# VectorE's order in the top-k attention of a Macaron block: where the sign word, the limits and the reciprocals stand

## The reference

```python
x = x + 0.5 * ffn(layernorm(x))       # x: 8 x 512 x 256
x = x + attn(layernorm(x))
x = x + 0.5 * ffn(layernorm(x))

def attn(x):                          # H = 16 heads of 64, 4 memory keys, TOPK = 64
    q, k, v = x @ Wq, x @ Wk, x @ Wv  # in heads; memory keys and values put in front of k and v
    q, k = l2norm(q), l2norm(k)
    dots = einsum('bhid,bhjd->bhij', q, k) * 10
    dots = einsum('hg,bgij->bhij', W_pre_th, dots)           # heads mixed before
    dots = where(causal, mask_value, dots)
    vk = top_k(dots, TOPK)[0][..., -1:]                      # the 64th largest of each row
    dots = where(dots < vk, mask_value, dots)
    attn = softmax(dots)
    attn = einsum('hg,bgij->bhij', W_post_th, attn)          # heads mixed after
    out = einsum('bhij,bhjd->bhid', attn, v) * head_scale
    return (out * sigmoid(x @ Wg + bg)) @ Wo
```

## Time and profile before

| | us |
|---|---|
| median of 3 runs | 2283.63 |
| lowest and highest of them | 2280.85 and 2287.51 |
| the profiled execution: time | 2286.81 |
| its span in the trace | 2285.0 |
| outside the span (2286.81 - 2285.0) | 1.81 |
| TensorE busy | 2040.8 (89%) |
| VectorE busy | 1765.2 (77%) |
| ScalarE busy | 1602.4 (70%) |
| GpSimd busy | 938.0 (41%) |

### The profile page before, as it was taken

How to read it: one execution, slowest core, us unless ns; L and a number is a source line. 1 busy time by engine, 2 the same in 40 slices (tenths; PEclk the granted TensorE clock), 3 DMA queues, 4 the chain that set the end, 5 groups by cost and what they waited for, 6 DMA issues and landing times. The chain is left out here.

```text
span 2285.0 us, 55636 instructions
## 1 busy us (share of the span) xinstructions
PE 2040.8 (89%) x16059; PEld 1325.7 (58%) x16060; DVE 1765.2 (77%) x6818; ACT 1602.4 (70%) x4676; POOL 938.0 (41%) x2739
## 2 busy tenths in 40 slices
PE   7995799899989998899899988998899889974997
PEld 3433456666666666666666666666666666663433
DVE  6565389968996899689968996899689958984346
ACT  4442589858985888589768875897689768951542
POOL 3001455454544554555355435553554356321000
PEclk9997799999999999999999999999999999997998
DMA  6002012111211121112111211121112101302002
GB/s 180 0 0 88 18 46 63 44 26 44 63 44 26 44 63 44 26 44 63 44 27 44 63 44 26 45 62 44 26 45 63 44 24 48 70 24 89 1 0 74
DMA packets 113219, 104.72 MB, mean 46 GB/s; under 512 B 34448, under 2 KB 110864, under 8 KB 112912
## 3 DMA queue, kind: packets, MB, share of 16 engines
q1 hardware_dynamic: 108000, 96.65, 16.6%
q10 hardware_dynamic: 4912, 4.46, 0.6%
HBM read 19.14 MB, written 12.71 MB: 14 GB/s over the span
## 5 line engine op out<-in xcount | busy, mean ns | idle before, releaser
L1054 PE MATMUL bankC<-R,E 128*128 128x128 f32 x2560 | 352.0, 287 | 46.9 <-POOL R L1416 46.9
L1054 PEld LDWEIGHTS bankC<-R,E 128*128 128x128 f32 x2560 | 338.3, 202 | 85.1 <-POOL R L1416 51.8
L1038 PE MATMUL bankB<-raw,mixpre 128*128 128x76 f32 (+37 forms) x1024 | 354.7, 434 | 20.4 <-DMA raw<-SC 20.3
L1254 ACT ACTIVATE S<-bankB,aim_first 128x68 f32<-128x68 f32 (+56 forms) x456 | 232.8, 514 | 87.8 <-PE bankB L1038 87.2
L1514 DVE TENSOR_SCALAR_CACHE_REDUCE S<-S,minus_thr 128x68 f32<-128x68 f32 (+56 forms) x456 | 217.7, 514 | 94.1 <-POOL minus_thr L1400 93.5
L1391 POOL TENSOR_TENSOR S<-S,diagmask 128x8 f32<-128x8 f32 x512 | 116.6, 233 | 409.1 <-ACT S L1254 353.0
L1568 DVE SCALAR_TENSOR_TENSOR E<-S,limit,E 128x68 f32<-128x68 f32 (+56 forms) x456 | 234.1, 549 | 37.6 <-ACT E L1280 9.0
L1416 POOL TENSOR_SCALAR R<-mixpost,rinv 128x128 f32<-128x128 f32 x512 | 187.6, 379 | 183.8 <-DVE rinv L1572 183.4
L1027 PE MATMUL bankD<-KT,QT 64*64 64x132 f32 (+8 forms) x2304 | 190.5, 405 | 66.5 <-ACT SC L1243 37.4
L1280 ACT ACTIVATE E<-S,nmax 128x12 f32<-128x12 f32 (+56 forms) x512 | 241.7, 535 | 0.0
L1080 PEld LDWEIGHTS bankM<-PT,V 128*64 128x64 f32 x5120 | 180.3, 138 | 97.9 <-issue 90.5
(11 more groups left out here) (178 smaller groups left out, 3927.7 us busy)
## 6 DMA issues: line engine op xcount, KB each, us to landing
X_first<-in_L_attn_x_dram ACTq DMA_DIRECT2D x8, 512.0 KB, 9.7
x<-X_first SPq DMA_DIRECT2D x8, 512.0 KB, 2.9
xt<-x SPq DMA_DIRECT2D x32, 128.0 KB, 2.3
x<-xt SPq DMA_DIRECT2D x32, 128.0 KB, 2.4
X_last<-x SPq DMA_DIRECT2D x8, 512.0 KB, 6.6
out_dram<-X_last SPq DMA_DIRECT2D x8, 512.0 KB, 2.8
raw<-SC SPq DMA_DIRECT2D x8, 258.0 KB, 3.0
raw<-SC SPq DMA_DIRECT2D x8, 254.0 KB, 3.0
```

The source lines that it names most:

```text
L1038: last = nc.tensor.matmul(bankB[n % 2][:, 0:wide(n)], W.mixpre[:, :], raw[n % RAWS][:, 0:wide(n)], start=True, stop=True)
L1054: last = nc.tensor.matmul(bankC[n % 2][:, jb * P:(jb + 1) * P], E[n % EBUFS][:, jb * P:(jb + 1) * P], R[n % RBUFS][:, :], start=True, stop ...
L1254: nc.scalar.activation(S[n % SBUFS][:, 0:wide(n)], src, ACT.Identity, bias=W.aim_first[:, group(n)]).then_inc(S_out, 1)
```

## The change

Four things are moved on VectorE's list; no other engine's list is touched.

1. The sign word (flip, L1527) was the first instruction of select_pair(n0), behind both row maxima. It becomes sides_pair(n0) and stands between row_max(n0+2) and row_max(n0+3).
2. The limit of both groups (L1556, one instruction) becomes one instruction for each group, each behind a wait for its own picked; the masked sum of a group waits for its own limit.
3. The reciprocal of a pair (L1572) was the last instruction of select_pair(n0). It becomes invert_pair(n0), and is called in the next iteration, behind row_max(n0+4) and before the next pair's sign word. So it also stands behind whatever follows select_pair(n0) in its own iteration: gate_half, ln_apply, residual, squares, mark_batch.
4. The reciprocal of the last pair stands behind the loop, so behind the last mark_batch. Its wait for R_ready (ring of 16) is put at the reciprocal too.

```diff
--- before.py
+++ after.py
@@ -1516,17 +1516,32 @@
                 else:
                     nc.vector.reduce_max(rmax[:, col(n)], row, axis=AX.X).then_inc(max_done, 1)
 
+            flipped, kept_sum = {}, {}
+
+            def sides_pair(n0):
+
+                ranked = ranked_in(n0)
+                if ranked:
+                    cols = ring(ranked)
+                    dve.wait_ge(side_done, ranked_upto(ranked[-1]))
+                    flipped[n0] = step(nc.vector.tensor_scalar(flip[:, cols], side[:, cols].bitcast(I32), 31, 0x7FFFFFFF,
+                                                               ALU.arith_shift_right, ALU.bitwise_or))
+
+            def invert_pair(n0):
+
+                both = (n0, n0 + 1)
+                dve.wait_ge(tk, kept_sum[n0])
+                if n0 >= RING:
+                    dve.wait_ge(R_ready, n0 - RING + 2)
+                nc.vector.reciprocal(rinv[:, ring(both)], rsum[:, ring(both)]).then_inc(E_ready, 2)
+
             def select_pair(n0):
 
                 both = (n0, n0 + 1)
                 ranked = ranked_in(n0)
                 at = {}
                 if ranked:
-                    cols = ring(ranked)
-                    dve.wait_ge(side_done, ranked_upto(ranked[-1]))
-                    flipped = step(nc.vector.tensor_scalar(flip[:, cols], side[:, cols].bitcast(I32), 31, 0x7FFFFFFF,
-                                                           ALU.arith_shift_right, ALU.bitwise_or))
-                    dve.wait_ge(tk, flipped)
+                    dve.wait_ge(tk, flipped[n0])
                     for n in ranked:
                         w = group_width(n)
                         at[n] = step(nc.vector.tensor_scalar(
@@ -1552,10 +1567,11 @@
                             out=picked[n % 2][:, :], in0=W.iotaM[:, :], scalar=order[:, col(n)], in1=top[n % 2][:, :],
                             op0=ALU.is_equal, op1=ALU.mult,
                             accum_out=key[:, parity(n), n % GPB:n % GPB + 1]).then_inc(picked_done, 1)
-                    dve.wait_ge(picked_done, ranked_upto(ranked[-1]))
-                    limited = step(nc.vector.tensor_tensor(
-                        limit[:, cols].bitcast(I32), key[:, parity(n0), in_batch(ranked)].bitcast(I32), flip[:, cols],
-                        ALU.bitwise_xor))
+                    for n in ranked:
+                        dve.wait_ge(picked_done, ranked_upto(n))
+                        at[n] = step(nc.vector.tensor_tensor(
+                            limit[:, col(n)].bitcast(I32), key[:, parity(n), n % GPB:n % GPB + 1].bitcast(I32),
+                            flip[:, col(n)], ALU.bitwise_xor))
                 for n in both:
                     w = group_width(n)
                     dve.wait_ge(exp_done, n + 1)
@@ -1563,13 +1579,12 @@
                         dve.wait_ge(R_ready, n - RING + 1)
                     least = MASKED / 2
                     if n in ranked:
-                        dve.wait_ge(tk, limited)
+                        dve.wait_ge(tk, at[n])
                         least = limit[:, col(n)]
                     at[n] = step(nc.vector.scalar_tensor_tensor(
                         out=E[n % EBUFS][:, 0:w], in0=S[n % SBUFS][:, 0:w], scalar=least, in1=E[n % EBUFS][:, 0:w],
                         op0=ALU.is_ge, op1=ALU.mult, accum_out=rsum[:, col(n)]))
-                dve.wait_ge(tk, at[n0 + 1])
-                nc.vector.reciprocal(rinv[:, ring(both)], rsum[:, ring(both)]).then_inc(E_ready, 2)
+                kept_sum[n0] = at[n0 + 1]
 
             def mark_batch(i):
 
@@ -1595,8 +1610,13 @@
             squares(1, 1)
             for n0 in range(0, NG, 2):
                 t, g = divmod(n0, GPT)
-                if 2 <= n0 and n0 + 2 < NG:
+                more = 2 <= n0 and n0 + 2 < NG
+                if more:
                     row_max(n0 + 2)
+                if n0:
+                    invert_pair(n0 - 2)
+                sides_pair(n0)
+                if more:
                     row_max(n0 + 3)
                 if g == 2 and t + 2 < NT:
                     ln_stats(t + 2)
@@ -1613,6 +1633,7 @@
                     squares(t + 1, 1)
                 if (n0 + 2) % GPB == 0:
                     mark_batch(n0 // GPB)
+            invert_pair(NG - 2)
             gate_half(NU - 2)
             gate_half(NU - 1)
             residual(NT - 2)
```

## The result

The changed kernel takes 2246.57 us (median of 4 runs, 2243.7 to 2247.8), the kernel before 2282.93 beside it. The ratio is 0.9836, with a 95% interval of 0.9818 to 0.9854: 36.4 us or 1.6% faster. The forecast was 12.5 us faster, 2271.1, with a range down to 2259. The sign was right, the size a third of what came. One of the six runs of e5_middle took 2637.43 us at a mean granted clock of 0.739, the five others 2271.79 to 2273.34 at 0.953 to 0.954; its ratio goes by those five.

What follows compares the result with a forecast made beforehand. VectorE was taken to set the time only in four iterations at each of 7 batch ends and the kernel's last 12; 9.1 + 3.4 = 12.5 us off 2286.81 gave 2274.3, as median 2271.1, range 2259 to 2283.

Steps and rivals of the forecast that it cites:

- the rival by which the time would rise to 2288: VectorE's list: order is free, only instruction count matters; one added limit an iteration costs 4.4 us; chance 0.05.
- the late R of group 58: Batch end: the put-off reciprocal gives TensorE R 0.76 us later, which fits into its wait for k of 1.87 to 2.92.
- the mask of group 5: GpSimd at a batch end: the later reciprocal just fits before this mask; up to 0.3 us a batch if it doesn't.
- an iteration: VectorE, each iteration: removed 0.34 + 0.20 + 0.05, added 0.11 + 0.15, so 0.33 us saved; ends 0.19 and 0.45.
- The slower rival: TensorE leads more and waits for the late reciprocal: 5.3 us at batch ends, 4.8 in wide tiles, 2294; chance 0.11.
- In tiles 1 and 2 nothing is gained: Middle of a batch: no gain; a later R taken as nothing, up to 0.3 us a tile on the bad side.
- a VectorE that works faster finds no thresholds to work on: Tile 2: VectorE and TensorE have no gaps to speak of, so VectorE's gain becomes longer threshold waits; size nothing.
- I take nothing: TensorE's clock at batch starts: loss of up to 1.7 us goes in five batches, counted as nothing; 8.5 kept as an end.
- the batches without it don't come to group 58 earlier in any regular way (they lose the clock elsewhere): Batches without the clock loss at their start: reason given for counting no time from its end.
- the clock comes along: Rival, TensorE's clock at batch starts: shorter waits end the clock loss, 8.5 us more, 2263; chance 0.12.
- the batch end: Group 58 to the squares: squares 1.35 us earlier; over 7 batch ends 5 x 1.35 + 1.11 + 1.25 = 9.1 us.
- The last batch: From group 42 of the last batch VectorE leads: 3.8 us gained, 0.3 to 0.4 back, net 3.4.

Runs made afterwards that it cites:

- e5_middle: All three moves only in the pairs of groups 0 to 54 of each batch, old order in 56 to 62, against the kernel before: ratio 0.9954.
- e3_limit: Only the limits split, one per group; reciprocal and sign word as in the kernel before: ratio 0.9915 to it.
- e8_recip58: The changed kernel with the reciprocal of groups 58 and 59 left right behind their masked sums: ratio 0.9839 to the kernel before.
- e9_last: All three moves only in the last batch (groups 448 to 511), the rest as in the kernel before: ratio 0.9957 to it.
- e7_delay: The changed kernel with four idle VectorE multiplications in front of the squares at each batch end: ratio 0.9906 to the kernel before.
- e10_tile2: All three moves only in pairs 32 to 47 (tile 2) of batches 0 to 6, against the kernel before: ratio 0.9977.
- e12_after: The changed kernel run again, unchanged, as a control: ratio 0.9851 to the kernel before.

## Why the prediction was wrong

**What held.** VectorE sets the time from group 58 to the squares; the squares come earlier, TensorE's wait for k shrinks and goes; the order of VectorE's list matters, not its count (the rival by which the time would rise to 2288 fell with e3_limit); no new wait of TensorE for R in tiles 1 and 2; the late R of group 58 fits into the wait for k; the mask of group 5 costs at most 0.12 us a batch (starts without a loss take 12.52 to 12.64 us, 12.52 and 12.53 before). The rule of the Trainium skill named beside that rival ("VectorE: DVE Perf Modes", "The DRAIN you can't avoid"), as the prediction tells it, doesn't agree with the trace: the maximum starts 0.00 us behind the read-out, and 0.53 us an iteration came from the order, with one instruction more. The prediction left out what the same section of the Trainium skill adds: a next op that is not held starts earlier. With that the trace agrees (the same 0.00 us). The slower rival had no place to bite: e8_recip58 shows the late R to be worth nothing either way, once all moves are made.

**Failed: "In tiles 1 and 2 nothing is gained", 11.2 us, of which some 5 are the order's and some 6 the clock's.** It was read from the busy shares, VectorE 55.22 and TensorE 55.91 of 57.81. Two engines that are both nearly full say nothing of which of them leads. The view that does was at hand: what VectorE's maxima wait for. These are the row maxima of groups 30 to 47 of batch 4, in the kernel before:

```profile
L1514 DVE TENSOR_SCALAR_CACHE_REDUCE S<-S,minus_thr x18: 469/544/615, 1237.6 to 1293.5; 128x252 f32<-128x252 f32 x1, 128x260 f32<-128x260 f32 x1, 128x268 f32<-128x268 f32 x1, 128x276 f32<-128x276 f32 x1
L1514 DVE DVE_READ_ACCUMULATOR S<-S,minus_thr x17: 81/83/86, 1238.0 to 1293.5; 128x1 f32 x17
its engine sat idle before it (us, times) until:
```

and in the kernel after:

```profile
L1514 DVE TENSOR_SCALAR_CACHE_REDUCE S<-S,minus_thr x18: 468/533/609, 1214.0 to 1268.9; 128x252 f32<-128x252 f32 x1, 128x260 f32<-128x260 f32 x1, 128x268 f32<-128x268 f32 x1, 128x276 f32<-128x276 f32 x1
L1514 DVE DVE_READ_ACCUMULATOR S<-S,minus_thr x18: 75/82/85, 1214.4 to 1269.4; 128x1 f32 x18
its engine sat idle before it (us, times) until:
  POOL minus_thr L1400: 1.2, 3
```

Before, nothing ended an idle time: VectorE waited for no threshold from group 28 to 54 of that batch. A faster VectorE could gain there, in the middle too. After, it waits at groups 32, 34 and 44. The step that failed is that a VectorE that works faster finds no thresholds to work on: e3_limit moves nothing but the limits, and at 0.99 its middles are 1.04 us shorter. But little of what VectorE saves comes through, 0.84 us a batch of some 22 iterations at 0.53. TensorE's idle time wouldn't have told how much: from group 32 to 48 of batch 4 it stood idle 1.11 us before and 1.10 after, while that stretch fell from 56.80 to 55.06. What caps the gain isn't shown.

**Failed, the largest: the clock, "I take nothing", 7.9 us at the starts and some 6 in the middle.** The loss was seen, its price (1.7) and its five places were right, and it was foreseen that shorter waits would end it. That "the batches without it don't come to group 58 earlier in any regular way (they lose the clock elsewhere)" was true of the kernel before, and e9_last bears it out. The step that failed is to carry this over to the changed kernel. There no other loss takes the place of the one at the start: all seven starts are free of it, no batch of 1 to 6 loses the clock between groups 52 and 58, and the middles stand at 0.99 or 1.00. In e7_delay and e5_middle the price appears in full. The rival "the clock comes along", 2263, was the nearest to the truth and got 0.12; it priced the starts alone.

**Mis-sized: an iteration, and with it the batch end, 14.0 for 9.1 us.** Reciprocal 0.26 for 0.23 (its place costs 0.08, not 0.11); sign word 0.15 for 0.05 (0.05, not 0.15); limits 0.12 for 0.05. Both places were priced by a row in which the instruction *behind* the reciprocal waited for its issue, 0.10 and 0.15. Between two maxima a 128x2 operation costs 0.05 to 0.08. My reading is that behind a maximum the waits of the next instruction are through already; no run tests it by itself. That makes 4 x 0.2 = 0.8 us more at the squares; another 0.40, at six of the seven, came from GpSimd's memsets, a term that the prediction didn't have. R of group 58 came 0.31 us later on average (16.97 for 16.66), not 0.76. So the gain of a batch end is TensorE's whole wait for k, 2.38 on average, less 0.31: 2.07, and 2.00 was measured. The k that it waits for is 2.0 to 2.5 us earlier.

**The last batch, 4.6 for 3.4 us.** From group 42 on, where the forecast began, it was 2.7; the other 1.9 come from groups 6 to 42. In the changed kernel run again this stretch took 201.99 us, a gain of 3.0, so the 3.4 lies within what one kernel scatters by.

In sum: 12.5 + 11.2 + 7.9 + 4.9 + 1.2 + 0.5 = 38.2, the budget without its last line. That the sign was right is no luck, since the batch ends were read rightly; the size missed the clock, the middle and the memsets.

## What to carry to other kernels

Where two engines are both over 95% busy, the shares don't say which leads: look at who waits for whom in that stretch, and don't set the gain of either to nothing. Before a stretch's gain is put down to a move, compare stretches at the same granted clock. A small operation whose result is waited for at once costs 0.2 to 0.34 us; the same operation between two wide ones on the same engine costs 0.05 to 0.08. A wait of TensorE behind which it loses the clock must be priced with the loss (1.8 to 1.9 us here) once the change shortens the wait; that the loss is made up elsewhere in the kernel before doesn't carry over.

## What the hardware showed that was not expected

- A clamp of 128x16 on VectorE took 0.58 us beside a GpSimd memset and 0.17 without, and ended 0.03 us behind the memset; a pass over 128x57 took 0.49 and 0.21.
- TensorE's clock (2.4 GHz, and 1.2 for a time after a wait): after 1.66 us of waiting the eight matmuls took 5.37 us in e7_delay, yet 3.67 after 1.87 and 2.01 us in the kernel before, and in e9_last 3.67 after 2.03, in e10_tile2 3.67 after 2.18. The length of the wait alone doesn't decide it; what does is open.
- The same kernel, after and e12_after, reached group 6 of batch 0 at 265.56 and 270.80 us. In the first the eight Wv matmuls from 254.07 took 3.67 us, in the second those from 256.30 took 6.68. Of the 14 profiled executions only after, e3_limit, e9_last and e10_tile2 have the 3.67 there.
